# Row maxima of an attention block: 64-row products in pairs on both halves of TensorE's rows

## The reference, cut to what matters

```python
q, k = split_heads(binlinear(x, Wq, bq)), split_heads(binlinear(x, Wk, bk))
att = einsum('bhtd,bhsd->bhts', q, k) * scale      # 16 heads of 8 channels
att = softmax(att, axis=-1)                         # needs each row's maximum
y = einsum('bhts,bhsd->bhtd', att, v)
```

## Time and profile before

| | |
|---|---|
| Median of 3 runs | 681.53 us (678.68 to 684.75) |
| The profiled execution | 685.48 us, its span 683.7 us |
| Granted TensorE clock, mean over the span | 0.971 |
| TensorE (matmul) busy | 624.5 us, 91% |
| VectorE busy | 516.7 us, 76% |
| ScalarE busy | 411.0 us, 60% |
| GpSimd busy | 264.0 us, 39% |

### The profile page before, as it was taken

The page is one execution under the profiler, slowest core; times in us unless marked ns, Lnnn a source line. Parts: engine busy times, 40 slices in busy tenths (PEclk is TensorE's granted clock), DMA queues, the critical chain, the costliest instruction groups (busy, mean ns, idle before and its releaser), DMA issues.

```text
span 683.7 us, 11593 instructions
## 1 busy us (share of the span) xinstructions
PE 624.5 (91%) x3693; PEld 298.9 (44%) x3693; DVE 516.7 (76%) x1104; ACT 411.0 (60%) x846; POOL 264.0 (39%) x309
## 2 busy tenths in 40 slices
PE   4988999999999999999999999999998898888935
PEld 2332333233333333433333333232465888888931
DVE  5659888889988989888898888983368655555617
ACT  2145777777777687777777777778542445444520
POOL 4221022324352461452434233134434366566540
PEclk9669999999999999999999999999999999999987
DMA  3533132222321233223222231115102222222228
GB/s 101 146 56 97 52 101 76 66 82 72 94 86 62 75 97 95 79 78 105 72 70 75 70 98 52 39 40 173 53 0 70 64 74 78 69 78 79 70 68 320
DMA packets 50064, 56.92 MB, mean 83 GB/s; under 512 B 10281, under 2 KB 39243, under 8 KB 50004
## 3 DMA queue, kind: packets, MB, share of 16 engines
q1 hardware_dynamic: 42648, 43.11, 22.4%
q0 software_dynamic: 4320, 8.47, 3.6%
q10 hardware_dynamic: 3036, 4.61, 2.1%
HBM read 38.36 MB, written 17.92 MB: 82 GB/s over the span
## 4 chain that ended last, share of the span: by engine, by line
PE 68%; DVE 13%; ACT 6%; DMA 4%; issue 4%; SPq 2%; POOL 1%; another core or an unknown queue 0%; ACTq 0%; POOLq 0%; DVEq 0%
PE pv L1457 15%; PE st L1446 14%; PE mx L1431 13%; PE st L1646 9%; DVE neg_max L1012 6%; PE mx L1590 3%; ACT pt L803 2%; PE misc L1324 2%; PE misc L1351 2%; PE pv L1655 2%; PE misc L1655 2%; PE st L1600 1%; PE misc L1357 1%; DMA even_qk<-k_parts 1%; DVE ln L969 1%
## 5 line engine op out<-in xcount | busy, mean ns | idle before, releaser
L803 ACT ACTIVATE pt<-st 128x512 f32<-128x512 f32 x496 | 282.2, 598 | 106.0 <-PE st L1446 96.8
L1012 DVE TENSOR_REDUCE neg_max<-mx 128x2 f32<-128x1024 f32 x248 | 294.4, 1215 | 50.5 <-PE mx L1431 47.3
L1457 PE MATMUL pv<-pt,vs 128*32 128x512 f32 x1024 | 136.4, 605 | 0.3 <-ACT pt L803 0.3
L690 POOL DMA_INDIRECT routed<-rec,row_u x64 | 64.4, 1007 | 142.1 <-PE pv L1457 115.2
L750 POOL DMA_INDIRECT results<-qs,home_u x71 | 77.4, 1091 | 60.5 <-ACT qs L932 42.1
L1446 PE MATMUL st<-even_qk 74*128 74x512 bf16 x256 | 88.9, 388 | 4.1 <-DMA even_qk<-m_rows 2.2
L1446 PE MATMUL st<-qs,ks 74*128 74x512 bf16 x240 | 81.5, 383 | 1.8 <-ACT pt L803 1.1
L1431 PE MATMUL mx<-even_qk 72*128 72x512 bf16 x240 | 74.5, 392 | 6.0 <-DVE neg_max L1012 3.4
L1431 PE MATMUL mx<-ks,qs 72*128 72x512 bf16 x256 | 76.5, 380 | 2.8 <-DVE neg_max L1012 2.5
L1258 DVE TENSOR_TENSOR vs<-vs,st 128x256 f32<-128x256 f32 x71 | 29.7, 418 | 42.6 <-ACT vs L927 31.4
L1646 PE MATMUL st<-vs,pt 128*128 128x128 f32 x376 | 52.0, 282 | 10.3 <-DVE vs L1258 7.4
(11 more groups left out here) (199 smaller groups left out, 792.7 us busy)
## 6 DMA issues: line engine op xcount, KB each, us to landing
ks<-routed SPq DMA_DIRECT2D x71, 65.0 KB
even_qk<-q_parts SPq DMA_DIRECT2D x48, 96.0 KB
qs<-q_parts SPq DMA_DIRECT2D x48, 96.0 KB
ks<-k_parts SPq DMA_DIRECT2D x48, 96.0 KB
even_qk<-k_parts SPq DMA_DIRECT2D x42, 96.0 KB
q_parts<-qk_parts SPq DMA_DIRECT2D x21, 128.0 KB
k_parts<-qk_parts SPq DMA_DIRECT2D x7, 384.0 KB, 2.3
x_in<-L_attn_x SPq DMA_DIRECT2D x8, 256.0 KB
```

The lines of the kernel that those rows point to most:

```text
L690: pool.indirect_dma_start(out=routed_dram, out_offset=bass.IndirectOffsetOnAxis(ap=row_u[:, k, t:t + 1], axis=0), in_=rec[b.par][:, k, t, ...
L803: act.activation(pt[n % 2][:, hh, :], score_bank(b, n, hh), ACT.Exp, scale=SCALE).then_inc(exp_done, 1)
L1012: dve.tensor_reduce(neg_max[g % 2][:, hh, 2 * half:2 * half + 2], mx_bank[half][:], AX_X, ALU.max, negate=True).then_inc(mx_free, 1)
L1457: last = pe.matmul(pv_bank[32 * hh:32 * (hh + 1), :], vs[b.par][:, j, HG * g + hh, :], pt[n % 2][:, hh, :], start=(n % Y_SLOTS == 0), stop ...
```

## The change

From fill 32 on (the second batch's first), a fill is one pair: head h on rows 0 to 63 and head h+2 on rows 64 to 127, for one block of 128 queries. The product has 64 rows instead of 72: the low part times the low part is left out of the maxima. The scores of the second pass keep all nine products. The upper half's operands lie in a new pair of buffers `upper`, loaded by six further DMAs for each group (`load_upper`). So that 64 rows hold the first eight products, the k parts are stored in another layout (three DMAs instead of one) and the q stack's rows are in another order. In the slots that have such fills, both are issued ahead of score 0 of the slot, right behind the weighted sums of the slot before. VectorE's list stays: first fill, side work, second fill.

```diff
+MAX_ROWS = PROD - DH
+PAIRS = HG // 2
...
+        upper = [sb(f"upper{i}", [P, 2, PAIRS, T], BF16) for i in range(2)]
...
+        def paired(f):
+
+            return f >= 2 * HG * G
...
+            def load_upper(b, g):
+
+
+                if b.const > 1 or g >= 2:
+                    sp.wait_ge(mx_full, 2 * HG * (G * b.n + g - 1))
+                h = HG * g + PAIRS
+                for i in range(PARTS):
+                    parts = PARTS - (i == PARTS - 1)
+                    r = P // 2 + i * PARTS * DH
+                    rows = slice(r, r + parts * DH)
+                    sp.dma_start(upper[g % 2][rows, 0], q_dram[b.par].rearrange("j d h t -> (j d) h t")[0:parts * DH, h:h + PAIRS, :]
+                                 ).then_inc(upper_loaded[g % 2], 16)
+                    sp.dma_start(upper[g % 2][rows, 1], part_rows(k_dram[b.par][i], h, PAIRS, parts)).then_inc(upper_loaded[g % 2], 16)
...
+                if pair == 0 and t == 0:
                     pe.wait_ge(stack_loaded[b.par][g], STACK_DMAS * (b.half + 1))
+                    if paired(f):
+                        pe.wait_ge(upper_loaded[g % 2], UPPER_DMAS * uppers(b, g))
+                pe.wait_ge(mx_free, f - 1)
...
+                pe.matmul(mx_bank[f % 2][:, 0, :], qs[b.par][0:MAX_ROWS, h, t * P:(t + 1) * P], ks[b.par][0:MAX_ROWS, h, :],
+                          start=True, stop=True)
+                rows = slice(P // 2, P // 2 + MAX_ROWS)
+                pe.matmul(mx_bank[f % 2][:, 1, :], upper[g % 2][rows, 0, pair, t * P:(t + 1) * P], upper[g % 2][rows, 1, pair, :],
+                          start=True, stop=True).then_inc(mx_full, 1)
...
                 for n in range(SLOTS):
                     g, j = n // TT, n % TT
                     fills = fills_at(b, n)
+                    together = bool(fills[0]) and paired(fills[0][0])
+                    if together:
+                        for f in fills[0] + fills[1]:
+                            max_scores(f)
...
                     scores(b, n, 0)
                     scores(b, n, 1)
-                    for f in fills[0]:
-                        max_scores(*fill_of(f))
+                    if not together:
+                        for f in fills[0]:
+                            max_scores(f)
                     between(b, n, first, last)
                     scores(b, n, 2)
...
                     scores(b, n, 3)
```

More of the change, by code:

```diff
@@ L197, in adaln_block @@
         gb_dram = nc.dram_tensor("gb_rows", (B, C), F32).ap()
-        k_dram = [nc.dram_tensor(f"k_parts{i}", (H, DH, PARTS, T), BF16).ap() for i in range(2)]
+        k_first = nc.dram_tensor("k_first", (H, DH, PARTS, T), BF16).ap()
+        k_dram = [nc.dram_tensor(f"k_parts{i}", (PARTS, DH, H, T), BF16).ap() for i in range(2)]
         w_loaded = [sem(f"w_loaded{i}") for i in range(2)]
@@ L239, in adaln_block @@
         stack_loaded = [[sem(f"stack_loaded{i}_{g}") for g in range(G)] for i in range(2)]
+        upper_loaded = [sem(f"upper_loaded{i}") for i in range(2)]
         misc_full = sem("misc_full")
@@ L333, in adaln_block @@
         STACK_DMAS = 16 * 2 * PARTS
+        UPPER_DMAS = 16 * 2 * PARTS
         BATCH_ROWS = 16 * K_TOP * TT
@@ L552, in body @@
             def body(b, first, last):
+                if not first:
+                    load_upper(b, 3)
                 spread_max(b, 1, use(b, "m1"))
@@ L556, in body @@
                 load_x_again(b)
+                if not last:
+                    load_upper(b.plus(1), 0)
                 spread_max(b, 2, use(b, "m2"))
@@ L561, in body @@
                     load_x(b.plus(3))
+                if not last:
+                    load_upper(b.plus(1), 1)
                 spread_max(b, 3, use(b, "m3"))
@@ L575, in body @@
                 if not last:
+                    load_upper(b.plus(1), 2)
                     spread_max(b.plus(1), 0, use(b, "m0"))
@@ L1424, in max_scores @@
                     return
-                if hh == 0 and half == 0:
+                if pair == 0 and t == 0:
                     pe.wait_ge(stack_loaded[b.par][g], STACK_DMAS * (b.half + 1))
-                if b.const > 0 or g > 0 or hh > 0:
-                    pe.wait_ge(mx_free, fill - 1)
-                for t in range(2):
-                    q0 = (2 * half + t) * P
-                    last = pe.matmul(mx_bank[half][:, t, :], qs[b.par][0:PROD, h, q0:q0 + P], ks[b.par][0:PROD, h, :],
-                                     start=True, stop=True)
-                last.then_inc(mx_full, 1)
+                    if paired(f):
+                        pe.wait_ge(upper_loaded[g % 2], UPPER_DMAS * uppers(b, g))
+                pe.wait_ge(mx_free, f - 1)
+                h = HG * g + pair
+                if not paired(f):
+                    for u in range(2):
+                        hu = h + PAIRS * u
+                        last = pe.matmul(mx_bank[f % 2][:, u, :], qs[0][0:PROD, hu, t * P:(t + 1) * P], ks[0][0:PROD, hu, :],
+                                         start=True, stop=True)
+                    last.then_inc(mx_full, 1)
+                    return
+                pe.matmul(mx_bank[f % 2][:, 0, :], qs[b.par][0:MAX_ROWS, h, t * P:(t + 1) * P], ks[b.par][0:MAX_ROWS, h, :],
+                          start=True, stop=True)
+                rows = slice(P // 2, P // 2 + MAX_ROWS)
+                pe.matmul(mx_bank[f % 2][:, 1, :], upper[g % 2][rows, 0, pair, t * P:(t + 1) * P], upper[g % 2][rows, 1, pair, :],
+                          start=True, stop=True).then_inc(mx_full, 1)
             def scores(b, n, hh):
@@ L1509, in _ @@
             for fill in range(FIRST_FILLS):
-                max_scores(*fill_of(fill))
+                max_scores(fill)
                 if fill == 1:
@@ L1562, in body @@
                     scores(b, n, 1)
-                    for f in fills[0]:
-                        max_scores(*fill_of(f))
+                    if not together:
+                        for f in fills[0]:
+                            max_scores(f)
                     between(b, n, first, last)
                     scores(b, n, 2)
-                    for f in fills[1][:1]:
-                        max_scores(*fill_of(f))
+                    if not together:
+                        for f in fills[1][:1]:
+                            max_scores(f)
                     scores(b, n, 3)
                     for f in fills[1][1:]:
-                        max_scores(*fill_of(f))
+                        max_scores(f)
                     if n > 0:
```

66 lines of the change are left out of this document (33 added, 33 removed).

## The result

The changed kernel takes 730.12 us (median of 4 runs, 725.89 to 736.19) where the kernel before, run beside it, takes 681.45 (678.68 to 684.75): a ratio of 1.072, 95% interval 1.062 to 1.082. It is slower by 48.7 us. The forecast was +30, at 711.5 us, with a range of 698 to 730: the measured median stands just above its end. The profiled execution took 732.77 us, its span is 731.0.

The account below looks back on a forecast made before the run. TensorE was taken as the bound at 98% busy, VectorE 11% behind; five full batches +20.9, batch 6 +4.3, batch 7's half +3.0 and batch 0's +1.8 made +30.0 on 681.5: 711.5 us, range 698 to 730.

Parts of the forecast that it names:

- The halves run together: TensorE's fills: two products as a pair cost 0.22 us instead of 0.44, removing 0.44 us in each of 112 slots.
- the rival: TensorE's halves don't run together: each head 0.44 us longer, floor 3.83, +67, 749 us in all; chance 0.08.
- A rule on loads: Second pair's loads would wait for the first pair, some 0.1 us a head, up to 11 us; the trace spoke against it.
- The floor: Slot without side work: ScalarE's chain of scores and exponentials in series with the pairs, 3.39 us where it was 3.04.
- VectorE in step with TensorE: Second fill waits for VectorE's previous slot: at least 2.59 us plus side work, binding in slots 1, 4, 5, 7, 9, 13.
- The wait for the projection: Slot 4: VectorE waits 0.53 us for TensorE's output projection after its first reduction.
- The seam's DMAs: Between two batches: stores and `upper` loads at most 0.77 us each on SyncE's queue, some 3.5 us left for landing.
- VectorE's side: Part on the second fill's wait for VectorE's reduction and side work, with slot lengths of 3.59 to 4.90 us.
- the list of signs: Expected in the profile after: TensorE busy about 80% at the same granted clock, slots near 3.4, a batch near 60 us.
- the small pieces: TensorE's small side work standing at slots' ends, about 0.1 and 0.15 us, 0.25 in a full batch.
- DMAs: no cost: Six more loads a group cost no time, their lateness covered at the seam of two batches.
- The faster rival: Pairs save what they promise because TensorE is the bound and its waits stay covered: 45 us less, 636; chance 0.07.

Follow-up runs that it names:

- e10: Changed kernel with extra TensorE products in the waits of slots 2, 5, 6 and 14, only where a wait is longer than they are: 718.25 us, ratio 1.049.
- e4: Changed kernel with its order and all its DMAs, but each fill two 72-row products one after the other: 740.93 us, ratio 1.109.
- e7: Changed kernel with both pairs between scores 1 and 2 instead of at the slot's head, VectorE's order unchanged: 692.75 us, ratio 1.013.
- e2: Changed kernel with VectorE reducing both fills of a slot before its side work: 676.57 us, ratio 1.012.
- e5: The changed kernel unaltered, run again in the second set: 724.27 us, ratio 1.065 to the kernel before.
- e11: The changed kernel unaltered, run in e10's set: 732.86 us, +46.4 on the kernel before's 686.48.
- e12: e8 with group 2's `upper` loads behind group 0's maxima and GpSimd's wait for scatters behind its modulation: 676.48 us, ratio 0.9908.
- e6: Changed kernel with pairs at the fills' old places and the next batch's group 1 `upper` loads behind group 3's maxima: 693.62 us, ratio 1.015.
- e1: Changed kernel with 17 extra 64-row TensorE products a batch in the waits of slots 2, 5, 6 and 14: 705.77 us, ratio 1.055.
- e8: Changed kernel with both pairs between scores 1 and 2 and VectorE reducing both fills before its side work: 682.82 us, ratio 0.9986.
- e3: Changed kernel with the pairs at the fills' old places, behind score 1 and behind score 2: 668.46 us, ratio 1.0044.

## Why the prediction was right in direction and short in size

Right, by its own steps, with what the undisturbed slots of e10 and of the changed kernel measured:

- **The halves run together.** Starts are 0.01 us apart, pairs 0.22. e4 gives the price of the rival, 0.33 a slot for the 0.44 assumed. A pair does not wait for the weights either: in the changed kernel the second pair's loads start with the first pair's products, at 336.90. The rule weighed under "A rule on loads" would have made the head longer; the trace disagrees with it, as the earlier trace rows did.
- **The floor.** It is 3.42 for 3.39: ScalarE's chain stands in series with the head. Its cause is shown by e7, where the same two pairs between scores 1 and 2 give 2.88.
- **VectorE in step with TensorE.** Slots 1, 4, 5, 7 and 13: 4.16, 4.97, 3.88, 3.65 and 4.50 measured, 4.16, 4.90, 3.89, 3.67 and 4.58 forecast. The wait for the projection was 0.49 for 0.53. The cause is shown by e2: with both reductions ahead of the side work all of it is gone.
- **The seam's DMAs.** TensorE lost nothing for them: the seam is 4.51 at full clock for 4.39 (the floor and 1.0). SyncE's queue shows the loads of `upper` at no more than was allowed: here of q 0.56 and 0.44, of k 0.75, where the bound was 0.77:

```profile
359.16 0.56 SPq L534 DMA_DIRECT2D upper<-q_parts  x1
359.76 0.75 SPq L536 DMA_DIRECT2D upper<-k_parts  x1
360.55 0.44 SPq L534 DMA_DIRECT2D upper<-q_parts  x1
```

**The step that failed** is in "VectorE's side" and in the list of signs, where the sum prices TensorE's waits as idle time and takes the rest "at the same granted clock". In the earlier trace rows one instruction of TensorE stands right behind the other; the change opens a wait of 1.38 us at the head of slot 5 and waits for ScalarE in every slot. The forecast counted TensorE's busy share of a batch down to 80% (88% by the profile, which counts both halves), and didn't ask what the clock makes of the waits. In the profiled execution TensorE ran at 1.2 GHz in seven stretches behind such waits, and its work there took nearly twice as long. Measured: 432.22 less 418.43 = 13.8 us, the same attention without and with (e10) TensorE held busy. In e5 and e11, with half as much of 1.2 GHz or less, it is 6.6 us. By medians the changed kernel stands 48.7, 40.3 and 46.4 us over the kernel before in its three sets, and in the last of them 31.8 with the waits filled. The Trainium skill, "TensorE: Matmul & The Clock Gate", A second HAM failure mode: psum-queue depth-cycling, describes TensorE idling between groups of products as it goes round PSUM banks, with its clock swinging between the two levels; the 0.50 of 317 to 321 us agrees with the swinging. That going round the `mx` banks does it no run here shows: the kernel before goes round the same banks at 1.00, and so does e2, which keeps the waits for ScalarE. The page was not weighed in the prediction.

The rest is of small sizes. The four stretches grew by 47.7 = 30.0 + 13.8 + 3.8, and the 3.8 can be read from e10's four stretches against the forecast's terms (27.4, 299.8, 58.5 and 28.9, together 414.6; measured 418.4). The floor's 0.03 in 112 slots makes 3.4. Slots 2, 12 and 15, at 3.48, 3.63 and 3.63, are some 0.3 in a batch over what the small pieces allowed, and slot 9 is 0.2 over in five batches. The other way, batch 7's half is 1.4 shorter, as its slot 7 lasts 1.98 where the sum took 3.67. That the sum came so near to e10 is in part luck, since these errors offset each other.

Slot 9 is the one small size with a mechanism that the traces show. It was forecast at 3.59 and measured at 3.46 to 4.28 in batches 1 to 5. Its cast takes 0.57 at most in the kernel before. In the changed kernel it is this at worst (timelines of GpSimd and VectorE, batch 4), and this at best (batch 3):

```profile
330.93 2.68 POOL L724 TENSOR_TENSOR rec<-ln,mod_now 128x512 f32<-128x512 f32 x2
...
331.27 1.22 DVE L402 CAST qk_parts<-qk_f 128x512 bf16<-128x512 f32 x1
...
267.71 0.41 DVE L402 CAST qk_parts<-qk_f 128x512 bf16<-128x512 f32 x1
...
267.77 1.50 POOL L719 TENSOR_TENSOR ln<-ln,mod_now 128x512 f32<-128x512 f32 x1 [4.46 <-POOLq L739]
```

GpSimd's modulation, late by its wait for scatters, runs beside the cast, which takes 1.22. The casts of batches 1 to 5 take 0.41, 0.85, 0.41, 1.22 and 0.65, and the slot lasts 3.46, 3.91, 3.69, 4.28 and 3.71. The times fit two engines that take turns. In the 14 traces there are 52 casts that start at least 0.14 us into a GpSimd instruction over 512 elements of a row and over 0.13 us before its end. All of them end 0.28 or 0.29 us behind the end of that instruction, whichever of GpSimd's lines it was. In the nine cases where the two start within 0.13 us of each other, as in batch 3, the cast keeps its 0.40 or 0.41 and GpSimd's instruction takes 1.41 to 1.66 instead of 1.26. The Trainium skill, "GPSIMD Engine Reference", 1. Specifications, states that GpSimd shares its SBUF interfaces with VectorE, with contention for some kinds of VectorE instructions; the casts here agree, though no run was made for it.

The cast is not all of it. In batch 3 it was short, and TensorE waited 0.52 for GpSimd's `rec` instead; in e2, where the cast stands behind both reductions, slot 9 still reaches 4.06, with a wait of 0.93 for `rec`. What both have in common is GpSimd's lateness. "DMAs: no cost" was right for the seam and missed this: GpSimd waits longer for its scatters, 15.8 us for 9.1. Where that wait was moved behind the work that TensorE needs (e12), slot 9 fell to 3.09, though three of its casts took 1.10 to 1.29.

**What stays open.** Why GpSimd waits longer for its scatters: the added loads are the obvious suspect, and e6, which moved some of them, brought the slot back but not the wait. What exactly brings the clock down, and why the stretches are 44, 20 and 17 us long in three executions of one kernel. The waits for ScalarE alone don't (e2), the waits of 1.38 us are followed by a stretch in 12 of 21 cases (the three executions of the changed kernel), and e7's six waits of 1.26 us in none. e1 and e10 fill four slots' waits at once, and no run separates them. Nor was the loss at batch 0's seam in e8 and e12 taken apart.

The faster rival was wrong for the reason given against it: the scores' wait for ScalarE doesn't shrink. e3 adds a second reason, for the old places: there the same saving goes into switches.

## What to carry to other kernels

Before taking work out of an engine that looks saturated, ask what that work was covering: here the fills stood in TensorE's waits for ScalarE, and put together at the head they left these waits bare and made the head longer. Two uses of a double buffer that become adjacent on the producer need their consumer's two steps adjacent too, or all that stands between them becomes the producer's wait. And a wait of TensorE can cost more than itself: price it once as idle time, and give a range for the work behind it at 1.2 GHz, since the same wait was followed by such a stretch in some batches and not in others. If a trace shows it, cheap products in the wait tell in one run how much it is.

## What the runs showed of the hardware that was not expected

- In the changed kernel, waits of 1.38 us in a TensorE that is busy for some 88% of the attention were followed by stretches at 1.2 GHz of 3.4 to 10.2 us in 12 of 21 cases. With six products in the wait the same slots ran at 2.4 GHz (e10), and six waits of 1.26 us in e7 were followed by none.
- Bfloat16 products of 512 columns over rows 0 to 63 and over rows 64 to 127 start 0.01 us apart or less and cost 0.22 for the two. Each change between 64-row halves and a 74-row product costs about 0.10 us, so one lone pair between full products saves nothing against two full products (e3).
- A VectorE cast of 128x512 from float32 to bfloat16 took 0.40 to 0.43 us alone. Started 0.14 us or more into a GpSimd instruction of 1.26 us, it ended 0.28 or 0.29 us behind that instruction's end, and took up to 1.42. Where the two started within 0.13 us of each other, the cast kept its time and GpSimd's instruction took 1.41 to 1.66.
- A scatter of GpSimd took 6.10 us from issue to landing in e8; the median of e3's 64 was 3.0.
